# A bidirectional Mamba written as four fixed lists of stages, one per engine

## The chip, the cores and the metric

One core of one Trainium2 chip runs the whole kernel in one launch. The metric is the device time of that core in microseconds (us), less is better. In the profile PE is TensorE (PEld its weight loads), DVE is VectorE, ACT is ScalarE, POOL is GpSimd, SP is SyncE with the DMA queues.

## The reference, cut to what matters

The input x has 4 sequences of 1024 tokens with 128 channels. It goes through a layer norm, a Mamba in both directions (forward on the tokens, backward on the reversed tokens, each with its own weights, the two outputs averaged and added to the residual), and then six layers of a local-attention transformer. One Mamba direction, with 256 inner channels and 16 states:

```python
def _mamba(x, W_in, W_conv, b_conv, W_x, W_dt, b_dt, A_log, Dp, W_out):
    xp, z = jnp.split(x @ W_in.T, 2, axis=-1)
    xc = silu(causal_depthwise_conv4(xp, W_conv) + b_conv)
    dt, Bm, Cm = jnp.split(xc @ W_x.T, [DT_RANK, DT_RANK + D_STATE], axis=-1)
    dt = jax.nn.softplus(dt @ W_dt.T + b_dt)
    A = -jnp.exp(A_log)
    # for every token t, with h of shape (256, 16):
    #   h = h * exp(dt_t * A) + (dt_t * xc_t) * B_t ;  y_t = sum over states of h * C_t
    y = ys + xc * Dp
    y = y * jax.nn.silu(z)
    return y @ W_out.T
```

The transformer is not shown; the change doesn't alter what it issues.

## The kernel before

Channels lie on the 128 partitions and tokens along the free dimension, so the 256 inner channels are two halves h = 0, 1. One pass s is one direction of one sequence (8 passes, even ones forward, odd ones backward). A pass has 16 steps n, one for each state; g = 16 s + n counts steps over the whole block, 128 of them. A step works on all 1024 tokens at once:

- TensorE spreads row n of B over all partitions with a matmul against a picked column (`b_rows`, through `rows`, L209) into a pair of PSUM banks, and row n of C (`c_rows`) into the other pair. ScalarE copies C to SBUF (`copy_c`, L316).
- ScalarE makes the decays exp(dt A_n) of both halves (`decays`, L309), up to four steps ahead.
- VectorE multiplies dt*xc by B for half 0 into the tile drive (L393) and for half 1 in place in PSUM (L395), and then runs one scan over the tokens for each half (L411), into one of four buffers of state.
- GpSimd multiplies each scanned state by C into read (L425).
- TensorE adds each read to y of its half with the identity as weights, in PSUM, over the 16 states (`add_read`, L229). y takes four of the eight banks for the whole block.

Once a pass come the projections of the next pass (`project` on TensorE, `take_projection` on ScalarE): x with the four taps of the convolution folded into the weights (L182), z (L188), x_dbl, which holds B, C and the low-rank dt (L196), and dt (L203), then softplus as Abs, Relu, Exp and Ln on ScalarE and a sum and a product on VectorE (L353, L360). B is split into a rounded and a low part (L346). At the end of a pass VectorE adds the skip term (L366, the old y in PSUM plus D times xc), multiplies by silu(z) (`gate`, L372), TensorE multiplies by W_out (L238), and VectorE adds half of the result to the residual (`add_output`, L380).

The order is written out in the loops: the tables say in which step each projection stands, in most cases for the whole 1024 tokens at once.

```python
PROJECT_AT = {1: ("x", 0, BOTH), 4: ("x", 1, [0]), 6: ("x", 1, [1]), 8: ("bc", 0, BOTH), 9: ("dt", 0, BOTH),
              10: ("dt", 1, BOTH), 12: ("z", 0, BOTH), 13: ("z", 1, BOTH)}
GATE_AT, OUTPUT_AT, SOFTPLUS_AT, SPLIT_AT, DT_AT, DTX_AT = 1, 2, 11, 10, 12, 14
LEAD_DECAYS = 3
```

The other four banks are two pairs, `slot[0]` and `slot[1]`. B of step g goes to `slot[g % 2]`; C of step g and the projection of step g go to `slot[(g + 1) % 2]`, one after the other, and B of step g+1 to the same one behind them. `take(q, now)` makes TensorE wait for the last reader of the pair. Each engine runs its instructions strictly in the order written.

## Time and profile before

| | before |
|---|---|
| median of 3 runs | 4172.57 us (4169.62 to 4175.07) |
| profiled execution: its time, its span | 4178.99 us, 4176.9 us |
| busy over the span: PE, DVE, ACT, POOL | 3828.7 (92%), 3409.8 (82%), 3048.1 (73%), 3035.9 (73%) us |
| granted TensorE clock, mean | 0.952 of full speed |
| Mamba block: TensorE's first matmul to the last output sum | 71.45 to 1232.35 us |

Busy is the time in which an engine has an instruction in work; the records of matmuls overlap a little at their ends. The granted clock is a mean over a stretch of two levels, 1.0 (2.4 GHz) and 0.5 (1.2 GHz). In lists of groups a row ends with the idle time of the engine just before those instructions and with what released them.

### The profile page before, as it was taken

Reading aid. Unit: us, or ns where it says so; the run is one execution under the profiler, and the core shown is the slowest. Engines: PE = TensorE matmul, PEld = TensorE weight load, DVE = VectorE, ACT = ScalarE, POOL = GpSimd, SP = SyncE. Lnnn points to the kernel's source line nnn. Section 1 sums busy time; section 2 is a strip of 40 time slices with the busy share of each in tenths; the row PEclk is TensorE's granted clock in tenths of the full one; section 3 lists DMA queues with packets and bytes.
Section 4 is the critical chain, followed back from the end, with each engine's and each line's share of the span. In section 5 each row is a group of like instructions: output and inputs, shape, how many; then the busy total and the mean of one; then the engine's idle time right before and its main releaser. Section 6 shows DMA issues by size and latency. Waiting matters only on the chain.

```text
span 4176.9 us, 110200 instructions
## 1 busy us (share of the span) xinstructions
PE 3828.7 (92%) x43616; PEld 2570.0 (62%) x43616; DVE 3409.8 (82%) x3480; ACT 3048.1 (73%) x6956; POOL 3035.9 (73%) x2330
## 2 busy tenths in 40 slices
PE   6788888888875999999999999999999999999998
PEld 2333333333333777777777777777777777777775
DVE  3788888888975888788887888788887888788885
ACT  4655645564534888788887888788887888788885
POOL 0455555554546888888888888888888888888883
PEclk8888898898887999999999999999999999999999
DMA  1000000000000000000000000000000000000001
GB/s 41 0 1 0 0 0 0 0 0 0 0 20 32 13 2 15 2 6 13 15 3 2 16 2 15 2 6 12 2 15 2 16 2 15 2 6 2 3 2 42
DMA packets 12012, 34.46 MB, mean 8 GB/s; under 512 B 2405, under 2 KB 4329, under 8 KB 10609
## 3 DMA queue, kind: packets, MB, share of 16 engines
q1 hardware_dynamic: 11504, 27.41, 1.9%
q8 instruction: 353, 5.78, 0.6%
q14 instruction: 155, 1.26, 0.1%
HBM read 23.21 MB, written 4.19 MB: 7 GB/s over the span
## 4 chain that ended last, share of the span: by engine, by line
PE 64%; issue 2%; ACT 1%; POOL 1%; DVE 0%; POOLq 0%; ACTq 0%; DVEq 0%
PE ps L849 16%; PE ps L779 12%; PE ps L838 9%; PE ps L790 8%; PE ps L826 6%; PE ps L874 5%; PE ps L887 3%; PE ps L811 1%; PE ps L801 1%; PE ps L856 1%; PE ps L862 1%; ACT prob L980 0%; PE ps L761 0%; ACT mixed L989 0%; POOL resid L1257 0%
## 5 line engine op out<-in xcount | busy, mean ns | idle before, releaser
L425 POOL TENSOR_TENSOR read<-state,c_row 128x1024 f32<-128x1024 f32 x256 | 598.9, 2359 | 620.7 <-DVE state L411 501.0
L1235 POOL TENSOR_TENSOR resid<-resid,sq 128x1024 f32<-128x1024 f32 x384 | 909.8, 2375 | 4.0 <-DVE sq L1089 3.7
L1257 POOL TENSOR_TENSOR resid<-resid,rnorm 128x1024 f32<-128x1024 f32 x384 | 725.5, 1905 | 17.8
L849 PE MATMUL ps<-mixed,w_vo 128*128 128x128 f32 x6144 | 718.6, 275 | 3.0 <-ACT mixed L989 2.3
L849 PEld LDWEIGHTS ps<-mixed,w_vo 128*128 128x128 f32 x6144 | 709.6, 192 | 12.9 <-issue 4.6
L779 PE MATMUL ps<-w_qk,xs_parts 128*128 128x512 f32 x2304 | 641.3, 414 | 47.3 <-issue 18.2
L980 ACT ACTIVATE prob<-ps,stat 128x64 f32<-128x64 f32 x3072 | 653.3, 384 | 1.1 <-DVE stat L1109 1.1
L229 PE MATMUL mamba_ps<-read,ident 128*128 128x512 f32 x1024 | 572.0, 697 | 22.4 <-DVE xc L366 19.8
L1089 DVE TENSOR_TENSOR sq<-ps,rope_l 128x1024 f32<-128x1024 f32 x384 | 462.7, 1205 | 119.1 <-ACT sq L942 118.8
L1102 DVE TENSOR_TENSOR resid<-ps,rope_l 128x1024 f32<-128x1024 f32 x384 | 464.5, 1210 | 74.6 <-ACT sq L942 67.5
L779 PEld LDWEIGHTS ps<-w_qk,xs_parts 128*128 128x128 f32 x2304 | 414.8, 192 | 164.0 <-issue 81.1
L942 ACT ACTIVATE sq<-ps 128x1024 f32<-128x1024 f32 x384 | 395.7, 1030 | 162.3 <-PE ps L779 127.0
L1264 POOL TENSOR_TENSOR prob<-prob,stat 128x1024 f32<-128x1024 f32 x192 | 366.2, 1907 | 174.9 <-DVE stat L1120 174.8
L989 ACT COPY mixed<-ps 128x512 f32<-128x512 f32 x768 | 399.5, 601 | 110.5 <-PE ps L838 110.5
L1066 DVE TENSOR_REDUCE ssq<-sq 128x16 f32<-128x1024 f32 x384 | 465.7, 1213 | 8.1 <-ACT sq L942 3.7
L790 PE MATMUL ps<-ident,resid 128*128 128x128 f32 x3072 | 413.9, 274 | 14.3 <-ACT w_vo L924 13.1
L229 PEld LDWEIGHTS mamba_ps<-read,ident 128*128 128x128 f32 x1024 | 209.1, 217 | 311.6 <-issue 262.1
L790 PEld LDWEIGHTS ps<-ident,resid 128*128 128x128 f32 x3072 | 350.9, 141 | 75.8 <-issue 61.1
L838 PE MATMUL ps<-prob_t,rows 32*128 32x512 f32 x3072 | 383.8, 613 | 4.2 <-DVE xb L1137 1.6
L316 ACT COPY c_row<-mamba_ps 128x1024 f32<-128x1024 f32 x128 | 128.4, 1003 | 270.9 <-PE mamba_ps L209 270.9
L964 ACT COPY q_t<-ps 128x512 f32<-128x512 f32 x384 | 230.4, 600 | 124.0 <-PE ps L790 121.7
L826 PE MATMUL ps<-k_t,q_t 64*32 64x64 f32 (+1 forms) x24576 | 291.6, 225 | 9.8 <-issue 9.3
(139 smaller groups left out, 6158.5 us busy)
## 6 DMA issues: line engine op xcount, KB each, us to landing
w_stage<-w_qk_hbm SPq DMA_DIRECT2D x6, 1024.0 KB, 4.9
vo_stage<-w_v_hbm SPq DMA_DIRECT2D x6, 512.0 KB, 3.8
vo_stage<-w_o_hbm SPq DMA_DIRECT2D x6, 512.0 KB, 4.6
xn<-x_hbm SPq DMA_DIRECT2D x4, 512.0 KB, 5.3
kept<-resid SPq DMA_DIRECT2D x8, 256.0 KB, 3.1
resid<-kept SPq DMA_DIRECT2D x8, 256.0 KB, 4.5
out_hbm<-resid SPq DMA_DIRECT2D x8, 256.0 KB, 2.0
w_stage<-w_hbm SPq DMA_DIRECT2D x6, 341.0 KB, 2.9
```

What stands on the lines that cost most here:

```text
L229: last = pe.matmul(y_ps[h][:, c, :], ident[:, :], read[:, (2 * g + h) % 4, c * BANK:(c + 1) * BANK], start=n == 0, stop=n == D_STATE - 1)
L425: pool.tensor_tensor(read[:, u % 4, :], state[:, u % 4, :], c_row[:, (u // 2) % 2, :], ALU.mult).then_inc(read_ready, 1)
L779: last = pe.matmul(ps[:, A + c, :], xs_parts[:, odd, xpart, :], w_qk[:, wpart, cols], start=k == 0, stop=k == 2)
L790: last = pe.transpose(bank[:, j * P:(j + 1) * P], qk[:, tile % 2, col:col + P], ident[:, :])
L826: last = pe.matmul(ps[w * WINDOW:(w + 1) * WINDOW, S + h, first:(a + 1) * 2 * WINDOW], q_t[rows_h, odd, a, w * WINDOW:(w + 1) * WINDOW], k ...
L838: last = pe.matmul(banks[w], rows[rows_w, tile % 2, own, :], prob_t[rows_w, tile % 2, :, own, :], start=own == 0, stop=own == 1)
L849: last = pe.matmul(bank[:, 0:P], w_vo[:, l % 2, head_at(place_h), :], mixed[:, odd, place_h, :], start=place_h == 0, stop=place_h == HEADS ...
L980: last = act.activation(prob[:, tile % 2, place_h, :], score_ps[:, place_h, :], ACT.Exp, bias=stat[:, tile % 2, 0, place_h:place_h + 1])
L1066: dve.tensor_reduce(ssq[:, tile % 2, part * HEADS:(part + 1) * HEADS, 0], sq[:, 0, :].rearrange("p (h d) -> p h d", d=HEAD_DIM), AX_X, ALU ...
L1102: dve.tensor_tensor(qk[:, tile % 2, part * INNER:(part + 1) * INNER].rearrange("p (h d) -> p h d", d=HEAD_DIM), heads_ps.rearrange("p (h d ...
L1235: pool.tensor_tensor(qk[:, tile % 2, cols], qk[:, tile % 2, cols], sq[:, 1 + part, :], ALU.add).then_inc(done[f"rotated{part}"], 1)
L1257: pool.tensor_tensor(heads, heads, norms, ALU.mult).then_inc(done[f"normed{part}"], 1)
```

## The change

The loops of the Mamba block are replaced by four lists, MAMBA_PE, MAMBA_ACT, MAMBA_DVE and MAMBA_POOL. An entry is (lag, step, stage): in round i the stage is issued for pass i - lag, so that work of up to three passes stands between one another in a list (`mamba_sequence`). Every stage waits for what it reads and for the last reader of what it overwrites (`after`, by counts taken from the lists).

- The four banks of the two pairs are given by `mamba_slots`: B still takes a whole pair, alternately; every other result (half of C, of x, z, x_dbl, dt or the output) takes one bank of the pair that B does not hold, the two in turn.
- C is spread and copied in two halves of 512 tokens (c0, c1; cc0, cc1), so are all projections and their reads, and the output with its sum (o0, o1; ao0, ao1).
- ScalarE reads x with Identity (bias added) and z with Copy, in halves, and then puts the whole of each channel half through Silu in SBUF (sx0, sx1, sz0, sz1). After a group of Silus it preloads the table set with Exp and Ln; one such preload stands at the start.
- Skip (gs0, gs1) and gate (gm0, gm1) stay on VectorE, as separate stages per half, and the identity sums (y0, y1) lag behind the scans by up to three steps.
- state and read have two buffers per half where they had four in turn. The semaphore `stored` of the transformer is allocated in `program` instead.

```diff
+MAMBA_PE = [
+    (2, 13, "c0"), (2, 13, "c1"), (2, 11, "y0"), (2, 14, "c0"), (2, 14, "b"), (2, 14, "c1"), (2, 12, "y0"), (2, 15, "b"),
+    (2, 11, "y1"), (2, 12, "y1"), (2, 15, "c1"), (2, 13, "y0"), (2, 15, "c0"), (2, 14, "y0"), (2, 13, "y1"), (1, 0, "b"),
+    (1, 0, "c1"), (2, 14, "y1"), (1, 0, "c0"), (2, 15, "y0"), (1, 1, "b"), (0, None, "x01"), (2, 15, "y1"),
+    (0, None, "x00"), (1, 1, "c1"), (1, 1, "c0"), (1, 2, "c1"), (1, 0, "y0"), (1, 2, "b"), (1, 2, "c0"), (2, None, "o0"),
+    (2, None, "o1"), (0, None, "z10"), (1, 0, "y1"), (1, 3, "b"), (1, 1, "y0"), (1, 3, "c0"), (1, 3, "c1"), (1, 2, "y0"),
+    (1, 4, "c1"), (1, 1, "y1"), (1, 4, "b"), (0, None, "x10"), (1, 4, "c0"), (1, 2, "y1"), (1, 5, "b"), (1, 3, "y0"),
+    (1, 5, "c1"), (0, None, "x11"), (1, 5, "c0"), (1, 4, "y0"), (1, 6, "b"), (1, 6, "c0"), (1, 3, "y1"), (1, 6, "c1"),
+    (1, 4, "y1"), (0, None, "z00"), (1, 7, "b"), (1, 7, "c0"), (0, None, "z01"), (1, 5, "y0"), (0, None, "z11"),
+    (1, 7, "c1"), (1, 5, "y1"), (1, 8, "b"), (1, 8, "c1"), (0, None, "bc1"), (1, 8, "c0"), (1, 6, "y1"), (1, 9, "b"),
+    (1, 6, "y0"), (1, 9, "c0"), (0, None, "bc0"), (0, None, "dt01"), (0, None, "dt00"), (1, 7, "y1"), (1, 10, "b"),
+    (1, 9, "c1"), (1, 8, "y1"), (1, 10, "c0"), (0, None, "dt11"), (1, 10, "c1"), (1, 7, "y0"), (1, 8, "y0"),
+    (1, 11, "b"), (1, 9, "y1"), (1, 11, "c1"), (1, 11, "c0"), (1, 9, "y0"), (1, 12, "b"), (1, 12, "c0"),
+    (0, None, "dt10"), (1, 12, "c1"), (1, 10, "y0"), (1, 10, "y1"), (1, 13, "b")]
+MAMBA_ACT = [
...
+    (2, 4, "cc1"), (1, None, "sx0"), (2, 6, "dec1"), (1, None, "ax10"), (2, 4, "cc0"),
...
+    (2, 6, "cc0"), (2, 6, "cc1"), (1, None, "sx1"), (1, None, "az00"), (2, 7, "cc0"), (1, None, "az01"),
+    (1, None, "sz0"), (2, None, "sz1"), (2, 7, "cc1"), (1, None, "az11"), (2, 9, "dec0"), (2, 8, "cc1"), (2, 8, "dec1"),
...
+MAMBA_DVE = [
+    (2, 14, "sc0"), (2, 14, "sc1"), (2, 15, "dr0"), (2, 15, "dr1"), (2, 15, "sc0"), (2, 15, "sc1"), (1, None, "tx1"),
+    (1, 0, "dr0"), (1, 0, "dr1"), (1, 0, "sc1"), (1, 0, "sc0"), (2, None, "gs0"), (1, 1, "dr0"), (2, None, "gm0"),
+    (1, 1, "dr1"), (2, None, "gs1"), (1, 1, "sc1"), (1, 1, "sc0"), (2, None, "gm1"), (1, 2, "dr0"), (1, 2, "dr1"),
+    (2, None, "ao0"), (1, 2, "sc0"), (2, None, "ao1"), (1, 2, "sc1"), (1, 3, "dr0"), (1, 3, "dr1"), (1, 3, "sc1"),
...
+    (1, 9, "dr0"), (1, 9, "dr1"), (1, 9, "sc1"), (1, 9, "sc0"), (0, None, "split"), (1, 10, "dr0"), (1, 10, "dr1"),
+    (1, 10, "sc0"), (1, 10, "sc1"), (1, 11, "dr0"), (1, 11, "dr1"), (1, 11, "sc0"), (1, 11, "sc1"), (0, None, "ar0"),
+    (1, 12, "dr0"), (1, 12, "dr1"), (1, 12, "sc0"), (1, 12, "sc1"), (0, None, "tx0"), (1, 13, "dr0"), (1, 13, "dr1"),
+    (1, 13, "sc1"), (1, 13, "sc0"), (0, None, "ar1"), (1, 14, "dr0"), (1, 14, "dr1")]
...
+def mamba_sequence(order):
+
+    out = []
+    for i in range(2 * BATCH + max(lag for lag, _, _ in order)):
+        for lag, n, name in order:
+            if 0 <= i - lag < 2 * BATCH:
+                out.append((name, i - lag if n is None else D_STATE * (i - lag) + n))
+    return out
...
+    slots, last, turn, pair = {}, [None] * 4, [0, 0], 1
+    for name, k in pe:
+        if name == "b":
+            pair = k % 2
+            banks, reader = [2 * pair, 2 * pair + 1], ("sc1", k)
+        elif name in single:
+            other = 1 - pair
+            banks, reader = [2 * other + turn[other]], (single[name], k)
+            turn[other] ^= 1
+        else:
+            continue
+        slots[name, k] = banks[0], sorted({last[q] for q in banks if last[q]})
+        for q in banks:
+            last[q] = reader
...
+        def after(eng, *producers):
+
+            for name, k in producers:
+                if k >= 0:
+                    eng.wait_ge(done[name], COUNT[name, k])
...
+                act.preload_act_table_set("natural_log_exp_and_others")
...
+                def copy_c(c):
+                    def stage(g):
+                        after(act, (f"c{c}", g), ("rd0", g - 2), ("rd1", g - 2))
+                        act.copy(c_row[:, g % 2, cols(c)], bank(f"c{c}", g)).then_inc(done[f"cc{c}"], 1)
+                    return stage
...
+                for i, (name, k) in enumerate(ACT_SEQ):
+                    stages[name](k)
+                    tables = [x[0] for x in ACT_SEQ[i + 1:] if x[0] in MAMBA_EXPS + MAMBA_SILUS]
+                    if name in MAMBA_SILUS and tables and tables[0] in MAMBA_EXPS:
+                        act.preload_act_table_set("natural_log_exp_and_others")
...
+                def scan(h):
+                    def stage(g):
+                        after(dve, (f"dec{h}", g), (f"dr{h}", g), (f"rd{h}", g - 2))
+                        force = pair(g).rearrange("p c n -> p (c n)") if h else drive[:, :]
+                        dve.tensor_tensor_scan(state[:, h, g % 2, :], decay[:, h, g % AHEAD, :], force,
+                                               0.0, ALU.mult, ALU.add).then_inc(done[f"sc{h}"], 1)
+                    return stage
```

## Rows read from the trace of the kernel before

**Rows 1.** Windows of the whole span by stage: busy time and instructions per engine, granted clock.
```profile
661.00:798.00 137.00, 118.49 (x243) 47.60 (x243) 114.08 (x70) 73.65 (x70) 72.13 (x31) 0.86 0.00 0
...
1400.00:4177.00 2777.00, 2709.32 (x40072) 2086.17 (x40072) 2302.21 (x2705) 2293.90 (x6077) 2334.21 (x1978) 0.99 0.03 9
```

**Rows 2.** Timeline of two steps without a projection, last pass: start, length, engine, operation.
```profile
1196.65 1.20 DVE L393 TENSOR_TENSOR drive<-dtx,mamba_ps 128x1024 f32<-128x1024 f32 x1
...
1197.45 3.90 PE L229 MATMUL mamba_ps<-read,ident 128*128 128x512 f32 x8
...
1203.56 1.19 DVE L393 TENSOR_TENSOR drive<-dtx,mamba_ps 128x1024 f32<-128x1024 f32 x1
```

**Rows 3.** Groups by line and shape, from 0 to 1500 us.
```profile
L229 PE MATMUL mamba_ps<-read,ident 128*128 128x512 f32 x1024 | 572.0, 697 | 22.4 <-DVE xc L366 19.8 <-POOL read L425 2.6
...
L209 PE MATMUL mamba_ps<-bc,pick_r 64*128 64x512 f32 x512 | 179.2, 447 | 131.2 <-DVE state L411 112.8 <-ACT c_row L316 14.5 <-ACT dtx L291 3.0
...
L309 ACT ACT_TABLE_LOAD x43 | 55.2, 1283 | 0.8
...
L277 ACT ACT_TABLE_LOAD x22 | 28.2, 1283 | 42.7 <-DVE zs L372 31.6 <-PE mamba_ps L182 10.8
...
L353 DVE TENSOR_TENSOR dt<-dt,dtx 128x1024 f32<-128x1024 f32 x16 | 20.1, 1295 | 15.2 <-ACT dt L300 15.2
L366 DVE SCALAR_TENSOR_TENSOR xc<-xc,packed,mamba_ps 128x1024 f32<-128x1024 f32 x16 | 19.8, 1275 | 4.5 <-PE mamba_ps L229 4.5
...
L360 DVE TENSOR_TENSOR dtx<-dt,xc 128x1024 f32<-128x1024 f32 x16 | 19.0, 1228 | 0.0
L372 DVE TENSOR_TENSOR zs<-xc,zs 128x1024 f32<-128x1024 f32 x16 | 18.8, 1218 | 0.0
...
L277 ACT ACTIVATE xc<-mamba_ps,packed 128x512 f32<-128x512 f32 x16 | 11.0, 687 | 53.8 <-PE mamba_ps L182 53.8
...
L380 DVE SCALAR_TENSOR_TENSOR resid<-mamba_ps,resid 128x1024 f32<-128x1024 f32 x8 | 9.8, 1225 | 19.4 <-PE mamba_ps L238 19.4
L346 DVE TENSOR_TENSOR bc<-x_dbl,bc 32x1024 fp32r<-32x1024 f32 x8 | 9.7, 1215 | 22.7 <-ACT bc L286 22.5
```

**Rows 4.** Waits from 100 to 1400 us: who waited for whom, us, times, longest.
```profile
DVE drive L393 <- PE mamba_ps L209: 125.3, 54, 7.0
...
DVE resid L380 <- PE mamba_ps L238: 19.4, 8, 4.4
```

**Rows 5.** Timeline of a step with a projection, pass 5.
```profile
714.94 3.59 PE L182 MATMUL mamba_ps<-xn,wtap 128*128 128x512 f32 x8
...
720.18 1.20 PE L209 MATMUL mamba_ps<-bc,pick_r 64*128 64x512 f32 x4
...
720.94 1.22 DVE L393 TENSOR_TENSOR drive<-dtx,mamba_ps 128x1024 f32<-128x1024 f32 x1 [1.62 <-PE mamba_ps L209]
```

**Rows 6.** Windows of 4 us, columns as in group 1.
```profile
677.00:681.00 4.00, 0.73 (x2) 0.29 (x2) 3.97 (x4) 1.01 (x1) 3.70 (x2) 0.82 0.00 0
681.00:685.00 4.00, 3.24 (x4) 1.51 (x5) 4.00 (x4) 0.00 (x0) 0.00 (x0) 0.50 0.00 0
...
689.00:693.00 4.00, 4.00 (x11) 1.75 (x10) 0.54 (x1) 0.08 (x1) 3.11 (x2) 1.00 0.00 0
```

**Rows 7.** Timeline of the preamble of the Mamba block.
```profile
71.45 15.93 PE L182 MATMUL mamba_ps<-xn,wtap 128*128 128x512 f32 x32 [15.37 <-DVE wtap L336]
...
104.79 1.28 ACT L297 ACT_TABLE_LOAD   x1
...
106.08 2.00 ACT L297 ACTIVATE dt<-dt 128x1024 f32<-128x1024 f32 x2
...
115.22 1.22 DVE L393 TENSOR_TENSOR drive<-dtx,mamba_ps 128x1024 f32<-128x1024 f32 x1
```

**Rows 8.** Timeline of the end of the Mamba block.
```profile
1215.20 2.25 DVE L411 TENSOR_TENSOR_SCAN state<-decay,mamba_ps 128x1024 f32<-128x1024 f32 x1
...
1231.12 1.23 DVE L380 SCALAR_TENSOR_TENSOR resid<-mamba_ps,resid 128x1024 f32<-128x1024 f32 x1 [4.39 <-PE mamba_ps L238]
```

More of the change, by code:

```diff
@@ L258, in _, with free, project_x, stage @@
-                for h in range(HALVES):
-                    add_read(STEPS - 1, h)
-                output(PASSES - 1, other_slot(STEPS - 1))
+                def free(name, k):
+                    after(pe, *SLOTS[name, k][1])
+                    return bank(name, k)
+                def project_x(h, c):
+                    def stage(s):
+                        to, d = free(f"x{h}{c}", s), s % 2
+                        for tap in reversed(range(D_CONV)):
+                            skip = max(0, D_CONV - 1 - tap - c * BANK)
+                            seen = tokens(s, c * BANK + skip - (D_CONV - 1 - tap), BANK - skip)
+                            last = pe.matmul(to[:, skip:], wtap[:, d, tap, h * P:(h + 1) * P], seen,
+                                             start=tap == D_CONV - 1, stop=tap == 0)
+                        last.then_inc(done[f"x{h}{c}"], 1)
+                    return stage
@@ new lines, in project_z, with stage, project_bc @@
+                def project_z(h, c):
+                    def stage(s):
+                        to = free(f"z{h}{c}", s)
+                        pe.matmul(to, win[:, s % 2, D_INNER + h * P:D_INNER + (h + 1) * P], tokens(s, c * BANK, BANK),
+                                  start=True, stop=True).then_inc(done[f"z{h}{c}"], 1)
+                    return stage
+                def project_bc(c):
+                    def stage(s):
+                        after(pe, ("sx0", s), ("sx1", s))
+                        to = free(f"bc{c}", s)
+                        for h in range(HALVES):
+                            last = pe.matmul(to[0:BC_ROWS + DT_RANK], wx[:, s % 2, h, :], xc[:, s % 2, h, cols(c)],
+                                             start=h == 0, stop=h == HALVES - 1)
+                        last.then_inc(done[f"bc{c}"], 1)
+                    return stage
@@ new lines, in b_rows, with c_rows @@
+                def b_rows(g):
+                    after(pe, ("split", g // D_STATE))
+                    free("b", g)
+                    for c in range(HALF_BANKS):
+                        last = rows(pair(g)[:, c, :], g, g % D_STATE, c)
+                    last.then_inc(done["b"], 1)
+                def c_rows(c):
+                    def stage(g):
+                        after(pe, ("split", g // D_STATE))
+                        rows(free(f"c{c}", g), g, D_STATE + g % D_STATE, c).then_inc(done[f"c{c}"], 1)
+                    return stage
@@ new lines, in output, with stage @@
+                def output(c):
+                    def stage(s):
+                        after(pe, ("gm0", s), ("gm1", s))
+                        to = free(f"o{c}", s)
+                        for h in range(HALVES):
+                            last = pe.matmul(to, wout[:, s % 2, h, :], zs[:, s % 2, h, cols(c)], start=h == 0, stop=h == HALVES - 1)
+                        last.then_inc(done[f"o{c}"], 1)
+                    return stage
+                stages = {**parts("x", project_x), **parts("z", project_z), **parts("dt", project_dt), **banked("bc", project_bc),
+                          "b": b_rows, **banked("c", c_rows), **halved("y", add_read), **banked("o", output)}
@@ L429 @@
+                stages = halved("rd", read_out)
+                for name, k in POOL_SEQ:
+                    stages[name](k)
 DEPTH, HEADS, HEAD_DIM, WINDOW = 6, 16, 64, 32
```

418 lines of the change are left out of this document (178 added, 240 removed), and 20 rows, old and new, of tables (MAMBA_ACT, MAMBA_DVE, MAMBA_POOL).

## The prediction

> **What bounds the kernel now.** I read the windows by stage first. The Mamba block is the part before 1232 us; from 1400 us on, the transformer keeps TensorE at 2709 of 2777 us at a granted clock of 0.99 [rows 1], and the diff touches nothing there that takes time (the semaphore `stored` is only allocated earlier). So 2,945 us of the 4,177 are the same in both kernels, and I ask only about Mamba. A typical window there has 137 us, of which VectorE is busy 114, TensorE 118 (at clock 0.86), ScalarE 74 and GpSimd 72 [rows 1]. Two engines are near full and neither is full: that is a pair of engines waiting for each other in turn.
>
> The timeline says which is the floor. In a step without a projection, the drive of half 0 comes back after 1203.56 - 1196.65 = 6.91 us, with nothing idle on VectorE (two drives and two scans), and TensorE has time left [rows 2]. At that pace 128 steps take 884.5 us. To them come the operations that occur once a pass: relu sum, product with xc, skip, gate, output sum and split, together 20.1 + 19.0 + 19.8 + 18.8 + 9.8 + 9.7 = 97.2 us, 12.15 a pass [rows 3]. Seven passes of these lie between the first drive at 115.22 [rows 7] and the end of the last scan at 1215.20 + 2.25 = 1217.45 [rows 8]: 85.1 us. VectorE alone would need 884.5 + 85.1 = 969.6 us; the stretch takes 1102.2. **132.6 us are stalls**, 137.8 us a pass where 122.7 would do at full packing. The view of waits names them: the drive waits 125.3 us for the B rows of L209, and the output sum 19.4 us for L238, 4.4 of it at the very end [rows 4, 8].
>
> Why are the B rows late? A pair of banks holds B(g-1) until its second scan ends. Then C(g), a whole projection and B(g+1) go through this same pair one behind the other, each after the ScalarE read of the one before. With a projection, eight matmul records take 3.59 us, and the next B comes 1.62 us late [rows 5]. I take 0.44 us for a record of 512 columns at full clock (3.59/8, a little off for the last one's drain), and 0.30 for a record of the row matmuls (1.20/4). The clock adds to it: TensorE is busy 0.73 of 4 us, the clock falls to 0.50 while VectorE is still fully busy, and two windows on VectorE is busy 0.54 of 4 us, waiting [rows 6]. Half speed is not paid in the light step where it arises, but in the heavy one that follows.
>
> **The change part by part.** *TensorE.* The same matmuls: 192 records a pass of 512 columns (128 of the identity sum, 1024 in all [rows 3], 32 of x, 8 each of z, bc, dt and output), and 64 row records [rows 3]. That is 192 x 0.44 + 64 x 0.30 = 103.7 us at full clock, against VectorE's 122.7. What moves is where they stand. A projection is now one bank (x 3.5 us, output and bc 1.8, z and dt 0.9), C is split in two single banks, and a turn within the pair lets one be computed while ScalarE reads the other. The identity sums lag up to three steps, so TensorE has work where it used to wait. I walked the steps of MAMBA_PE with these durations, t = 0 where the other pair comes free. B is ready at 4 to 5 us in steps 3, 4, 8 and 11, of the 6.9 that VectorE gives; at 6.2 to 6.6 in steps 5, 6 and 10; near 7.1 in step 7 (z01, z11 and sz0, sz1 of ScalarE). Steps 1, 2, 9 and 12 hold the most, and there VectorE has its extra 1.2 to 5 us (gs0, gm0, gs1, gm1; two ao; split; ar0 and tx0), so B is in time by 1 to 2 us. That leaves under 1 us of stall a pass at full clock. One record at half clock costs 0.44 more, and steps 5, 6, 7 and 10 have no more than 0.7 to spare; one such stretch a pass costs some 2 us. I take **3 us a pass, 22 in all**, between 0 and half of the present stalls, 66.
>
> *VectorE.* Same operations in the same number, except that the output sum is cut in two. No row shows a 512-wide output sum; ScalarE's reads cost 0.69 for 512 columns, so two are 1.38 where VectorE's whole one is 1.23 [rows 3]. That is 0.15 more a pass, 1 us. Drives now name their operands as two banks of 512; the same 1024 elements lie in the same order, so I put 0, and if it did cost, the difference of the two kinds of drive-like operation here (1.23 against 1.30 [rows 3]) times 256 bounds it at 18 us. The scan's order (half 1 first in some steps) costs nothing of itself; GpSimd follows in the same order.
>
> *ScalarE.* More reads, in halves: C twice 0.6 to 0.69 for 1.0, x and z read first by Identity or Copy and then put through Silu in SBUF. That adds some 5 us of C, 2.5 of x, 2.5 of z and 1 of dt, say 11 a pass. Fewer table loads: sx0 stands alone, sx1, sz0 and sz1 share one, and a preload of the set with Exp and Ln follows each group, so four a pass where 88 stand now (43 and 22 of them in two rows [rows 3]): 11 a pass, so minus 7 x 1.28 = 9 us. ScalarE goes from about 75 to under 80 of 122.7 us: not a bound, hidden behind VectorE, as GpSimd's 72 is [rows 1]. But it is a strict list, and its waits (dec for the scan four back, cc for rd two back, abc for the previous dt) now hold what stands behind them: the worst place is sx1, load and Silu 2.3 us before az00, for which B of step 7 waits.
>
> On the price of a load the trace and the Trainium skill differ. In the preamble the load takes 1.28 us, and the activation starts at 106.08, right behind it [rows 7]. ScalarE: Activation LUTs, section "What ACT_TABLE_LOAD costs", has the same load and a drain of 1.38 us besides. By the page seven loads fewer would be 19 us of ScalarE a pass and not 9; the measurement decides, and since ScalarE is covered either way the sum is the same.
>
> *The preamble.* TensorE starts at 71.45 and the first drive at 115.22 [rows 7]. In the new list ScalarE's items of pass 0 up to the first decays are 16 halves of 0.69, 9 whole ones of about 1.1 and two loads of 1.28: 23.5 us. The first x bank before them, the waits of bc and dt on each other, and add, product and drive behind them add some 8. That gives 103 to 105 if no turn is missed. The gain lies between 2.6 (two loads) and 13; I take **10**, since nothing covers a new wait here.
>
> *The end.* From the last scan to the last output sum it is now 1232.35 - 1217.45 = 14.9 us [rows 8]. The gate of half 0 moves ahead of the skip of half 1, and the first bank of the output is added while the second is computed: **2** less, between 0 and 4.
>
> Sum: 132.6 - 22 - 1 + 10 + 2 = 121.6, rounded to 122. The profiled execution took 4178.99 us with its span of 4176.9, so 2.1 lie around it, and it is 6.4 over the median of 4172.57; the gain is 2.9% either way. 4172.6 - 122 = **4050 us**.
>
> **The rivals.** *(A) Only half the stalls go (0.15).* If the lists, whose slack is 0.3 to 0.7 us in four steps, meet the clock's falls, each pass keeps 8 of its 16 us of waits. For it: those falls are in the present rows [rows 6]. Against it: TensorE's work is spread. 66 + 10 = 76: 4097 us.
>
> *(B) The bound moves and nothing is gained (0.03).* B would have to be late by 16 us a pass, 1 us in every step, with ScalarE's added reads as the cause. It would need ScalarE near full, and it has over 40 us a pass free. 4173 us.
>
> *(C) TensorE becomes the bound and the kernel gets slower (0.05).* One mechanism: pieces of one bank, each behind a wait for its reader, leave TensorE so many short gaps that the clock stays low. TensorE needs 103.7 us over the clock; it equals today's 137.8 at a clock of 0.75, and above that point it does not decide. At 0.70 it takes 148 a pass, plus 10 x 8: 4255 us. The rows give 0.86 with gaps of 3 us and more [rows 1, 6], and the new list has less idle time to share out, so a small chance. The Trainium skill has this as a rule: TensorE: Matmul & The Clock Gate, "A second HAM failure mode: psum-queue depth-cycling", tells of a kernel that went through its banks in turn and whose clock swung because of short idle times between groups. By that rule (C) would happen; the trace agrees that the clock swings, but shows it after gaps of several us.
>
> *(D) No stall remains (0.07).* 132.6 - 1 + 13 + 4 = 149: 4024 us, the least that VectorE's floor allows.
>
> **How the numbers follow.** The forecast has 0.70: 4050, by itself 4030 to 4073 (1 to 6 us of stall a pass). The range takes in (D) and (A): 4023 to 4098. What a measurement of this kernel can tell from no change is about 0.2%, 8 us. Forecast, (A) and (D) are faster: 0.92. (B) is the same: 0.03. (C) is slower, 0.05.
>
> **What would show it.** After: a pass of 123 to 127 us between like scans; VectorE busy 96% of a window in the passes; its wait for the B rows 125.3 -> about 20; the clock in a pass at 0.93 or more; some 33 table loads in Mamba; first drive at about 105; the transformer from its start to its end as long as before. It would be wrong if waits of VectorE appear elsewhere (for `dec`, `rd` or `y`), if ScalarE is over 95 us a pass, or if the clock in the passes is under 0.8.

## The result, and the profile after

The changed kernel takes 4157.19 us (median of 7 runs, 4147.51 to 4162.93) against 4174.53 of the kernel before on the same chips: a ratio of 0.9959, 95% interval 0.9945 to 0.9972. It is faster by 0.4%, where 2.9% was forecast, and lies far above the range. The profiled execution has a span of 4161.1 us, 15.8 less than before.

Cut at the same four places in both traces (first drive of half 0, end of the last scan, end of the last output sum, end), the spans stand like this; the last column is the sum of the prediction:

```
                                   before     after    change   forecast
start to first drive               115.22    111.30      -3.9      -10
first drive to last scan          1102.23   1052.35     -49.9     -109.6
last scan to last output sum        14.90     16.24      +1.3       -2
last output sum to the end        2944.51   2981.16     +36.7        0
span                              4176.9    4161.1      -15.8     -121.6
```

Mamba's steps gave less than half of what was expected, and the transformer, in which no arithmetic is changed, became 37 us longer.

**The windows by stage**, to be read beside [rows 1] (columns as there):

```profile
661.00:798.00 137.00, 122.84 (x264) 47.60 (x265) 129.30 (x79) 76.52 (x96) 93.50 (x33) 0.94 0.00 0
...
1400.00:4161.00 2761.00, 2666.97 (x39391) 2048.89 (x39389) 2265.40 (x2660) 2245.70 (x5956) 2285.91 (x1942) 0.99 0.03 8
```

In the pass VectorE is now busy 129 us of 137 (94%, where 96% was forecast), and TensorE has a granted clock of 0.94, as forecast. But GpSimd is busy 94 us, where it was 72, for about as many reads (33 and 31 instructions in the windows).

**VectorE's waits**, to be read beside [rows 4]:

```profile
DVE drive L471 <- PE mamba_ps L307: 51.4, 43, 4.7
DVE state L479 <- ACT decay L417: 8.2, 7, 1.6
```

The wait for the B rows fell from 125.3 to 51.4 us, and 8.2 for the decays came up; 22 had been allowed.

**The groups by line and shape**, with the instruction's mean in ns after the busy time:

```profile
L521 POOL TENSOR_TENSOR read<-state,c_row 128x1024 f32<-128x1024 f32 x256 | 725.8, 2856 | 442.0 <-DVE state L479 246.4 <-PE mamba_ps L330 104.3 <-ACT c_row L424 90.8
...
L479 DVE TENSOR_TENSOR_SCAN state<-decay,drive 128x1024 f32<-128x1024 f32 x128 | 322.8, 2522 | 0.0
L479 DVE TENSOR_TENSOR_SCAN state<-decay,mamba_ps 128x1024 f32<-128x1024 f32 x128 | 290.1, 2267 | 11.0 <-ACT decay L417 8.2 <-POOL read L521 0.4
...
L495 DVE TENSOR_TENSOR zs<-xc,zs 128x1024 f32<-128x1024 f32 x16 | 34.1, 2134 | 0.1
```

The same groups in the kernel before:

```profile
L425 POOL TENSOR_TENSOR read<-state,c_row 128x1024 f32<-128x1024 f32 x256 | 598.9, 2359 | 620.7 <-DVE state L411 501.0 <-ACT c_row L316 119.7
...
L411 DVE TENSOR_TENSOR_SCAN state<-decay,drive 128x1024 f32<-128x1024 f32 x128 | 299.5, 2340 | 0.2
L411 DVE TENSOR_TENSOR_SCAN state<-decay,mamba_ps 128x1024 f32<-128x1024 f32 x128 | 289.1, 2259 | 0.0
```

GpSimd's read took 2359 ns before, now 2856. The scan of half 0, all of whose operands are in SBUF, took 2340, now 2522. The scan of half 1, whose force is in PSUM, is where it was (2259, now 2267). And the gate, two SBUF operands as well, went from 1218 [rows 3] to 2134. Nothing in the diff changes what these instructions do.

**The timeline at step 3 and step 4 of one pass** shows what an instruction is waiting for when it is long:

```profile
670.94 2.29 DVE L479 TENSOR_TENSOR_SCAN state<-decay,mamba_ps 128x1024 f32<-128x1024 f32 x1
...
675.49 4.68 POOL L521 TENSOR_TENSOR read<-state,c_row 128x1024 f32<-128x1024 f32 x2 [2.59 <-DVE state L479]
...
677.81 4.51 DVE L479 TENSOR_TENSOR_SCAN state<-decay,drive 128x1024 f32<-128x1024 f32 x1
...
682.25 2.25 DVE L479 TENSOR_TENSOR_SCAN state<-decay,mamba_ps 128x1024 f32<-128x1024 f32 x1
```

The scan of half 1 comes first in step 3 on VectorE, but GpSimd's list has the read of half 0 first there. So GpSimd starts its two reads at 675.49, once both scans are over, and they last until 680.17. VectorE's next scan of half 0 begins at 677.81 and takes 4.51 us: 2.28 and the 2.2 until GpSimd is done. An engine that waits for a semaphore shows idle time; this one shows a longer instruction.

Which engine pays is not fixed here. In step 4 this scan and GpSimd's second read start within 0.02 us of each other in all eight passes. In five of them the scan took 4.5 us and the read 2.35; in the other three the scan took 2.28 and the read 4.43.

**The timeline of one step in which no VectorE instruction is lengthened**, between two drives of half 0 (the scans take 2.28 and 2.26 us; it is GpSimd's read beside them that takes 4.41):

```profile
755.41 1.21 DVE L471 TENSOR_TENSOR drive<-dtx,mamba_ps 128x1024 f32<-128x1024 f32 x1
...
762.05 1.20 DVE L471 TENSOR_TENSOR drive<-dtx,mamba_ps 128x1024 f32<-128x1024 f32 x1
```

6.64 us, where [rows 2] had 6.91. Part of that 6.91 had been waits too. In the kernel before each half-1 drive waited for the half-0 drive before it to be finished (a start-to-start of 1.24 us, now 1.13). And the half-0 scan of that one step was 0.15 us longer than 2.28, beside a read that lasted until 1199.31:

```profile
1199.03 2.43 DVE L411 TENSOR_TENSOR_SCAN state<-decay,drive 128x1024 f32<-128x1024 f32 x1
```

The commonest step of the kernel before took 6.77 us.

**The preamble and the end:**

```profile
71.84 9.20 PE L276 MATMUL mamba_ps<-xn,wtap 128*128 128x512 f32 x16 [15.36 <-DVE wtap L440]
...
77.72 0.69 ACT L360 ACTIVATE xc<-mamba_ps,packed 128x512 f32<-128x512 f32 x1 [6.29 <-PE mamba_ps L276]
...
111.30 1.22 DVE L471 TENSOR_TENSOR drive<-dtx,mamba_ps 128x1024 f32<-128x1024 f32 x1
```

The first bank of x is in ScalarE's hands 5.9 us after TensorE's start, and ScalarE then waits for TensorE before each of the other three x banks too (2.67, 0.66 and 2.75 us); the prediction had some 8 us for the first bank and all waits up to the first drive. The end:

```profile
1161.39 2.26 DVE L479 TENSOR_TENSOR_SCAN state<-decay,mamba_ps 128x1024 f32<-128x1024 f32 x1
...
1161.54 8.85 PE L330 MATMUL mamba_ps<-read,ident 128*128 128x512 f32 x20
...
1168.71 1.28 DVE L487 SCALAR_TENSOR_TENSOR xc<-xc,packed,mamba_ps 128x1024 f32<-128x1024 f32 x1 [5.05 <-PE mamba_ps L330]
...
1179.20 0.69 DVE L508 SCALAR_TENSOR_TENSOR resid<-mamba_ps,resid 128x512 f32<-128x512 f32 x1 [2.25 <-PE mamba_ps L340]
```

Five groups of lagging sums (20 records) stand in front of the skip, which begins 5.1 us after the last scan.

**The transformer.** A run of 128 matmuls of 64 columns (L826 before, L927 after) in the changed kernel:

```profile
1290.79 1.12 PE L927 MATMUL ps<-k_t,q_t 64*32 64x64 f32 x91
1293.14 0.63 PE L927 MATMUL ps<-k_t,q_t 64*32 64x64 f32 x37 [1.23 <-issue]
```

Nothing is being waited for (issue), yet TensorE stands still for 1.23 us between two equal instructions. TensorE's waits that end in "issue" on this line, over the whole transformer, after and before (us in total, times, longest):

```profile
PE ps L927 <- issue: 37.5, 39, 1.9
```

```profile
PE ps L826 <- issue: 9.3, 22, 1.8
```

Counted in all of TensorE's records (weight loads, matmuls and the waits between them), these pauses stand at one place in every 256: within the runs of 64-column matmuls no other instruction starts more than 0.4 us behind the one before it. I summed the start-to-start times in front of the instructions of one residue modulo 256, over the transformer: the median over all residues is 11.0 to 11.3 us in these traces; at the residue with the pauses it is 28.9 us before and 64.2 after. The difference, 35.3, is nearly all of the transformer's 36.7. Most boundaries cost nothing: of the 192 that fall into such runs 40 cost more than 0.3 us (26 before), and none of these lies in the first two thirds of a run. In the last fifth they cost 1.0 us on average, 0.3 before; some stand just behind a run, in front of L939 (up to 1.4 us).

### The profile page after: what moved, and what is told of

It reads as the page before. It is cut to its first block, busy times and chain, and to the rows that moved or that the text cites. A ratio compares the mean times of both kernels' runs of the same rounds, so it can differ in the third digit from the quotient of the medians.

```text
span 4161.1 us, 111723 instructions
## 1 busy us (share of the span) xinstructions
PE 3836.6 (92%) x43616; PEld 2552.7 (61%) x43616; DVE 3442.0 (83%) x3488; ACT 3023.3 (73%) x7123; POOL 3160.4 (76%) x2330
## 4 chain that ended last, share of the span: by engine, by line
PE 65%; issue 2%; ACT 1%; POOL 1%; DVE 0%; POOLq 0%; ACTq 0%; DVEq 0%
PE ps L950 16%; PE ps L880 13%; PE ps L939 9%; PE ps L891 8%; PE ps L927 6%; PE ps L975 5%; PE ps L988 3%; PE ps L912 1%; PE ps L902 1%; PE ps L957 1%; PE ps L963 1%; ACT prob L1081 0%; PE ps L862 0%; ACT mixed L1090 0%; POOL resid L1358 0%
## 5 line engine op out<-in xcount | busy, mean ns | idle before, releaser
L521 POOL TENSOR_TENSOR read<-state,c_row 128x1024 f32<-128x1024 f32 x256 | 725.8, 2856 | 442.0 <-DVE state L479 246.4
L950 PEld LDWEIGHTS ps<-mixed,w_vo 128*128 128x128 f32 x6144 | 708.2, 192 | 12.7 <-issue 4.6
L330 PE MATMUL mamba_ps<-read,ident 128*128 128x512 f32 x1024 | 546.0, 665 | 2.7 <-POOL read L521 2.7
L1043 ACT ACTIVATE sq<-ps 128x1024 f32<-128x1024 f32 x384 | 395.2, 1029 | 168.4 <-PE ps L880 136.5
L424 ACT COPY c_row<-mamba_ps 128x512 f32<-128x512 f32 x256 | 145.8, 583 | 362.7 <-PE mamba_ps L307 312.4
L939 PE MATMUL ps<-prob_t,rows 32*128 32x512 f32 x3072 | 389.1, 615 | 7.2 <-issue 3.2
L330 PEld LDWEIGHTS mamba_ps<-read,ident 128*128 128x128 f32 x1024 | 192.9, 204 | 240.1 <-issue 232.3
L927 PE MATMUL ps<-k_t,q_t 64*32 64x64 f32 (+1 forms) x24576 | 294.3, 225 | 37.6 <-issue 37.5
L479 DVE TENSOR_TENSOR_SCAN state<-decay,drive 128x1024 f32<-128x1024 f32 x128 | 322.8, 2522 | 0.0
```

Source lines behind the costliest of these rows:

```text
L330: last = pe.matmul(y_ps[h][:, c, :], ident[:, :], read[:, h, g % 2, cols(c)], start=n == 0, stop=n == LAST)
L521: pool.tensor_tensor(read[:, h, g % 2, :], state[:, h, g % 2, :], c_row[:, g % 2, :], ALU.mult).then_inc(done[f"rd{h}"], 1)
L927: last = pe.matmul(ps[w * WINDOW:(w + 1) * WINDOW, S + h, first:(a + 1) * 2 * WINDOW], q_t[rows_h, odd, a, w * WINDOW:(w + 1) * WINDOW], k ...
L939: last = pe.matmul(banks[w], rows[rows_w, tile % 2, own, :], prob_t[rows_w, tile % 2, :, own, :], start=own == 0, stop=own == 1)
L950: last = pe.matmul(bank[:, 0:P], w_vo[:, l % 2, head_at(place_h), :], mixed[:, odd, place_h, :], start=place_h == 0, stop=place_h == HEADS ...
```

## The experiments

Segments of all runs, cut as above. "Pauses" is the sum at every 256th instruction, "shift" how many instructions stand in front of the transformer more than in the kernel before, modulo 256.

```
                      first    to last   to output   to the   pauses  shift
                      drive     scan       sum         end            mod 256
before               115.22   1102.23     14.90     2944.51    28.9      0
after                111.30   1052.35     16.24     2981.16    64.2    150
e1 short reads       110.47   1007.83     16.25     2977.40    57.2    150
e2 straight order    111.88   1100.21     20.07     2977.09    55.5    150
e3 clear of reads    112.16   1096.99     20.35     2977.16    60.1    150
e4 after, +106       119.91   1045.71     16.25     2936.12    20.2      0
e5 before, +150      116.10   1102.36     14.91     2985.85    59.6    150
e6 after, +106       110.75   1039.37     15.53     2939.84    23.0      0
e7 gate moved, +106  111.07   1018.84     16.39     2938.95    22.4      0
e8 short sums        109.30   1024.87     10.86     2983.39    63.3    150
e9 B first, +106     109.97   1033.96     17.55     2943.20    23.5      0
e10 after, +256      109.55   1048.77     16.26     2997.76    60.1    150
e11 after, +234      109.27   1041.65     13.83     2990.37    59.9    128
e12 B13 first, +106  109.50   1010.30     17.40     2942.07    24.6      0
```

Each line is one trace. In five of them Mamba's instructions are the same (after, e4, e6, e10, e11), and its stretch from the first drive to the last scan lies between 1039.4 and 1052.4 us. A part of that spread is step 4 above: the scan is the one that waits in 5, 1, 1, 4 and 4 of the 8 passes. So a difference of less than 13 us between two such stretches doesn't show an effect.

### The transformer: e4, e5, e6, e10, e11

The instructions put in are waits on a semaphore that has long been raised; two of them make one instruction.

```diff
 # e5: in the kernel before; e6, e10, e11: in the changed kernel, with 212, 512, 468
         @block.tensor
         def _(pe):
+            for _ in range(300):
+                pe.wait_ge(GATE[0], 2)
```

**e4**: the same in front of Mamba's first matmul, 212 waits.

> The changed kernel with 106 instructions more on TensorE's queue (waits on a semaphore long satisfied) before its first matmul of Mamba, where it waits 15 us for the taps. With the 406 that the change adds, the transformer's instructions are then shifted by 512, a multiple of 256, against the kernel before. In both traces the transformer's extra idle time stands at every 256th instruction of TensorE (28.9 us before, 64.2 after, against 11.0 at any other residue). Theory F1 (where the transformer's instructions lie against these blocks of 256 decides): the time from the last output sum of Mamba to the end goes from 2981 back to about 2945 us, total about 4121. Theory F2 (the length of these pauses hangs on something else, such as where the program lies in memory or the single execution): it stays within 10 us of 2981, or moves without regard to the shift.

4120.40 us, ratio to before 0.9870 (0.9856 to 0.9885). The rest fell by 45 us to 2936.12, and the pauses by 44.0; 8.6 us went to the instructions themselves, which outlasted the idle time before the first drive.

> The kernel before with 150 instructions more on TensorE's queue, at the very start of the transformer, where it waits over 25 us for weights (so they lie in idle time): waits on a semaphore long satisfied. 150 is what the change's 406 leave modulo 256. Theory F1 (the position against the blocks of 256 decides): the time from the last output sum of Mamba to the end goes from 2945 to about 2980 us, and the kernel is 30 to 40 us slower, about 4208, with Mamba as before. Theory F2 (a property of the changed program or of its place in memory): no change, 4173.

4218.11 us, ratio 1.0104 (1.0088 to 1.0119). The kernel before, with nothing but 150 more instructions in idle time (the first projection starts 0.3 us later than without them), loses 41 us in the transformer, and Mamba stays at 1102.4. 30.7 of the 41 stand at the boundaries; the other 10 are spread over the transformer and not explained. Its pauses on this line (L831 there):

```profile
PE ps L831 <- issue: 34.1, 34, 1.8
```

> The changed kernel with the 106 instructions at the start of the transformer, in idle time, and not before Mamba's first matmul, where they put the first drive off by 8 us. Theory F1: rest 2936 to 2945 us as in the run with the shift before Mamba, first drive back at 111, total 4112 to 4116. F2: about 4157.

4108.02 us, ratio 0.9843 (0.9825 to 0.9862), 49 us below the changed kernel's median. In the traces the rest is 41.3 us shorter and the pauses 41.2; another 13 stand in Mamba, where nothing is changed. The pauses on the same line (L932 there):

```profile
PE ps L932 <- issue: 4.8, 10, 1.8
```

> The changed kernel with 256 instructions at the start of the transformer on TensorE's queue. Theory F1 (position modulo 256): nothing changes against the changed kernel, rest 2977 to 2986 us and the idle time at each 256th instruction 55 to 65 us. Theory F3 (position modulo more than 256, or simply any shift from the present place): the rest falls to about 2940.

> The changed kernel with 234 instructions there, half a block (128) beyond e6. Theory F1 says only that 64 and 60 us stood at a shift of 150 modulo 256 and 20 to 29 at a shift of 0, so a shift of 128 should give a value near that of 150: 45 to 65 us at each 256th instruction and a rest of 2965 to 2985.

e10: 4174.11 us in one run, pauses 60.1. A whole block of 256 leaves them as they were, so the residue counts. Its rest, expected as before, is 16.6 us over that of the changed kernel. 11.8 of them are there because the first projection of the transformer starts 61.6 us after the last output sum and not 49.8: the 256 instructions, one every 0.107 us, last longer than the idle time. e11: 4156.91 us in one run, pauses 59.9, first projection at 59.2, so its rest is 5 us over the expected 2985 as well. A shift of half a block is as bad as one of 150; only the position of the kernel before was good, of the three that were tried.

Theory F1 holds in both directions and F2 and F3 fall: two programs with the same arithmetic differ by some 40 us in the transformer by where its TensorE instructions lie against blocks of 256. Why boundaries in the last fifth of a run cost 0.3 us at one position and 1.0 at the other, though about as many of them fall there (35 and 38), no run shows.

### GpSimd and VectorE: e1

```diff
-                        pool.tensor_tensor(read[:, h, g % 2, :], state[:, h, g % 2, :], c_row[:, g % 2, :],
+                        pool.tensor_tensor(read[:, h, g % 2, 0:64], state[:, h, g % 2, 0:64], c_row[:, g % 2, 0:64],
                                            ALU.mult).then_inc(done[f"rd{h}"], 1)
```

The one memset of read that the run also has is not shown.

> The changed kernel, but GpSimd's 256 reads multiply 64 of the 1024 columns (the other columns of the read tile stay at 0 from one memset before), so y is not computed in full; all else, the waits too, is the same. Theory P (a VectorE instruction with two SBUF inputs and a GpSimd multiplication of two SBUF operands exclude each other, and each waits for the other in turn; the late reads then make the identity sums and B late): the half-0 scan goes from 2.52 us back to 2.28 and the gate from 2.13 to 1.2, VectorE's wait for the B rows falls from 51 us to under 20, and the stretch from first drive to last scan falls from 1052 us to about 985. Theory Q (B is late because of TensorE's own list and its clock, and the long VectorE instructions only fill time that would be waited out): the durations fall as well, but the waits for B grow by as much, and the stretch stays above 1035.

4111.87 us, ratio 0.9851 (0.9832 to 0.9871). The half-0 scan by form, and VectorE's wait for B:

```profile
L479 DVE TENSOR_TENSOR_SCAN state<-decay,drive 128x1024 f32<-128x1024 f32 x128 | 291.7, 2279 | 0.0
```

```profile
DVE drive L471 <- PE mamba_ps L307: 61.5, 51, 4.6
```

The scan is back at 2279 ns, the gate at 1211, and the stretch is 44.5 us shorter. That is theory P's first half. Its second half is wrong: the wait for B did not fall to under 20 us but rose to 61.5, and the stretch is 1008, not 985. Theory Q foresaw the waits and put the stretch too high. So the long instructions cost about 45 us and were not hidden: VectorE's instructions in the stretch add up to 44.6 us less, while its waits of over 0.15 us stay at 63 in total (10 more for B, 10 less for decays and outputs).

And B is late by itself as well. For step 6, with 12.7 of the 61.5 us, this trace shows why. A window from the drive of step 5 to that of step 6 (columns as in [rows 1]):

```profile
405.46:414.09 8.63, 8.63 (x21) 3.33 (x19) 6.70 (x6) 3.16 (x5) 0.64 (x2) 1.00 0.00 0
```

TensorE is busy in all of the 8.63 us, at a granted clock of 1.00, while VectorE needs 6.70 of them. It is the same in three other passes. The list gives TensorE more to do before this B than the step lasts.

### The order of the scans and the gate: e2, e3, e7

```diff
 # e2: steps 0, 1, 3, 9 and 13 of MAMBA_DVE, MAMBA_POOL to match
-    (1, 0, "sc1"), (1, 0, "sc0")
+    (1, 0, "sc0"), (1, 0, "sc1")
 # e3: besides e2; the first three lines are also e7, there with (1, 1, "sc1"), (1, 1, "sc0") kept
-    (2, None, "gs0"), (1, 1, "dr0"), (2, None, "gm0"), (1, 1, "dr1"), (2, None, "gs1"), ... (2, None, "gm1"),
+    (1, 1, "dr0"), (2, None, "gs0"), (1, 1, "dr1"), (2, None, "gs1"), (2, None, "gm0"), (2, None, "gm1"), ...
+    MAMBA_PE: (1, 1, "b"), (2, 15, "y1"), (0, None, "x01")
+    MAMBA_PE: (1, 4, "b"), (1, 2, "y1"), (0, None, "x10"); (1, 9, "c0"), (1, 9, "c1"), (0, None, "bc0")
+    MAMBA_ACT: (2, 9, "cc0"), (2, 9, "cc1"), (2, 9, "dec1")
```

> The changed kernel with the scans of half 0 before those of half 1 in all steps (five steps a pass had them the other way), and GpSimd's reads in the same order. Theory P: in a step with half 1 first, the read of half 1 can't start while the scan of half 0 runs, both reads stand behind it and meet the next half-0 scan; in order, the reads fall under the half-1 scan and the drives, which have a PSUM operand. The half-0 scan falls to under 2.4 us and the stretch by 20 to 35 us, total about 4130. Theory Q: half 1 first frees the PSUM pair 2.2 us earlier for the x banks of steps 1 and 4 and for step 10, so B comes later in these steps: waits for B grow by up to 2.2 us in three steps a pass, and the total is 4150 to 4180.

> As the straight order, and besides: skips and gates stand after the drives of step 1 (dr0, gs0, dr1, gs1, gm0, gm1), where both reads are over; y1 of the last step goes ahead of x01, y1 of step 2 ahead of x10; both halves of C of step 9 are made before B of step 10. Theory P: the gate is back at 1.2 to 1.3 us, VectorE's total excess is under 10 us, waits for B under 20: stretch 990 to 1010, total 4105 to 4125. Theory Q: total as with the straight order alone, within 8 us.

e2: 4208.06 us, ratio 1.0083 (1.0068 to 1.0098). e3: 4207.18, ratio 1.0082 (1.0065 to 1.0099). Both are slower than the kernel before, and my theory about the order falls. The half-0 scan and the gate in e3:

```profile
L479 DVE TENSOR_TENSOR_SCAN state<-decay,drive 128x1024 f32<-128x1024 f32 x128 | 355.8, 2780 | 0.0
...
L495 DVE TENSOR_TENSOR zs<-xc,zs 128x1024 f32<-128x1024 f32 x16 | 18.8, 1219 | 0.0
```

The gate is at 1219 ns, because it stands where no read runs; but the half-0 scans became longer, 2780 ns, not shorter. Summed over the passes, their excess over 2280 ns is 31 us in the changed kernel, 52 in e2 and 64 in e3. The straight order doesn't take GpSimd's reads from under the half-0 scans, because they are late for another reason too: GpSimd waits for the identity sums that free its buffers, 104.3 us in the changed kernel, 168.4 in e2 and 200.6 in e3. These sums stand in TensorE's list behind the x banks, which in e2 get their PSUM pair one scan later; that this is the link is argued from the lists and not shown by a run. The five swapped steps are not the fault of the change; taken back without the rest of the plan, they cost 48 us of the stretch.

> As e6, and in step 1 skips and gates stand after the drives (dr0, gs0, dr1, gs1, gm0, gm1), y1 of the last step goes ahead of x01; the scans keep the change's order, half 1 first in five steps. Theory P with its first part alone (what the gate waits for GpSimd is lost on VectorE's path): gate from 2.13 to 1.2 us, 15 us less than e6. Theory Q' (VectorE's time saved there comes back as a wait for B, since TensorE and ScalarE have little to spare in the steps behind): gate 1.2 us, total within 5 us of e6.

4090.09 us, ratio 0.9799 (0.9785 to 0.9814), against e6's 4108.02 on the same chip. The gate is at 1217 ns and the stretch 20.5 us shorter than e6's. Theory P holds here, Q' falls: the 18 us between the medians are at least the 14.6 that the 16 gates had lost. The sum y1 that e7 also moves ahead of x01 was not tested by itself.

### TensorE's work: e8

```diff
 # e8: besides e1
-                            last = pe.matmul(y_ps[h][:, c, :], ident[:, :], read[:, h, g % 2, cols(c)],
+                            w = BANK if n == 0 else 64
+                            last = pe.matmul(y_ps[h][:, c, 0:w], ident[:, :], read[:, h, g % 2, c * BANK:c * BANK + w],
```

> As e1 (GpSimd multiplies 64 columns), and TensorE's identity sums take 64 of 512 columns except in the first state of a pass, so both y and the output are not computed; TensorE then has some 45 us less work a pass. In e1 VectorE still waited 61 us for the B rows. If these waits are TensorE's work (theory T), they fall under 15 us and the stretch from first drive to last scan from 1008 to 950 to 965. If they are ScalarE's list and its waits (theory A), they stay above 40 and the stretch above 990.

4130.19 us in one run, 18 more than e1 with less work. A window of one pass (columns as in [rows 1]) and the wait for B:

```profile
250.00:387.00 137.00, 110.76 (x276) 56.32 (x274) 125.97 (x81) 79.31 (x101) 16.62 (x33) 0.68 0.00 0
```

```profile
DVE drive L472 <- PE mamba_ps L307: 71.6, 51, 4.6
```

The wait rose from 61.5 to 71.6 us, and the stretch to 1024.9. The granted clock fell to 0.68 from e1's 0.94: TensorE, with less to do, was at 1.2 GHz for most of the window. Neither T nor A can be read from that; the run doesn't separate TensorE's work from ScalarE's list, because it changed the clock.

### B behind the sums: e9, e12

The wait for B by step in e7, summed over the passes (all idle time of VectorE before the half-0 drive, gaps under 0.15 us too, which the view of waits leaves out): step 13 has 19.3 of 53.9 us, step 6 has 11.5. The timeline of e7 at step 13:

```profile
715.35 16.74 POOL L524 TENSOR_TENSOR read<-state,c_row 128x1024 f32<-128x1024 f32 x5 [2.68 <-PE mamba_ps L333]
...
729.31 6.28 PE L333 MATMUL mamba_ps<-read,ident 128*128 128x512 f32 x8
...
733.26 2.35 POOL L524 TENSOR_TENSOR read<-state,c_row 128x1024 f32<-128x1024 f32 x1 [1.17 <-PE mamba_ps L333]
...
735.51 1.19 PE L310 MATMUL mamba_ps<-bc,pick_r 64*128 64x512 f32 x4
...
736.28 1.22 DVE L474 TENSOR_TENSOR drive<-dtx,mamba_ps 128x1024 f32<-128x1024 f32 x1 [3.04 <-PE mamba_ps L310]
```

GpSimd ends the fifth of its reads at 732.09 and needs 3.35 us for each, where a free one takes 2.36. TensorE's sums from 729.31 on contain y1 of step 10, which waits for it, and B of step 13 (735.51) stands behind. VectorE drives at 736.28, 3.04 us late.

```diff
 # e9 and e12: MAMBA_PE
-    (1, 10, "y0"), (1, 10, "y1"), (1, 13, "b")]
+    (1, 10, "y0"), (1, 13, "b")]       and (2, 10, "y1") at the head of the list
 # e9 alone
-    (1, 5, "c0"), (1, 4, "y0"), (1, 6, "b"),
+    (1, 5, "c0"), (1, 6, "b"), (1, 4, "y0"),
```

> As e7, and on TensorE's list B of step 13 stands ahead of y1 of step 10, and B of step 6 ahead of y0 of step 4. In the trace of e7 these two steps hold 19.3 + 11.5 of VectorE's 54 us of waits for B, and in step 13 TensorE stands at y1 of step 10, whose read GpSimd delivers late (five reads in 16.7 us for 11.8), with B ready to be made behind it. Theory P (late reads hold up B through TensorE's order): the waits in steps 6 and 13 fall from 31 to under 10 us and the total from 4090 by 12 to 22, to 4068 to 4078. Theory A (the reader of B's bank on ScalarE, relu10 or ax11, comes as late anyway): the waits stay above 20 and the total within 5 us of e7.

4106.51 us, ratio 0.9818 (0.9797 to 0.9839). Step 13 is down to 1.0 us and step 6 to 5.7, but step 7 rose from 4.7 to 18.6, and the excess of the half-0 scans from 16.3 to 32.5. The expected 12 to 22 us did not come; what two waits gave stands in other places. One of its five runs took 4083.96 us, the others 4104 to 4107.

> As e7, with only B of step 13 ahead of y1 of step 10 (the other exchange of e9, in step 6, is taken back). In e9 the wait in step 13 fell from 19.3 to 1.0 us, that in step 7 rose from 4.7 to 18.6, and the excess of the half-0 scans rose from 16 to 33 us. If the exchange in step 6 was to blame for both (its y0 came later, and GpSimd's reads with it), this kernel keeps 15 us of e7's waits and comes to 4072 to 4080. If VectorE, going on earlier in step 13, only meets GpSimd's late reads in its next scans (theory P: the two engines hand the delay to one another), the excess in steps 13 and 14 rises by some 14 us as in e9 and the total stays within 5 us of 4090.

4081.05 us (4071.34 to 4096.35), ratio 0.9776 (0.9756 to 0.9796), the lowest median of all, but its interval overlaps that of e7. VectorE's wait for B in e7 and in e12:

```profile
DVE drive L474 <- PE mamba_ps L310: 50.3, 41, 4.7
```

```profile
DVE drive L474 <- PE mamba_ps L310: 27.3, 29, 4.6
```

23.0 us less are waited for B, the excess of the half-0 scans is 9.7 us more (26.0), and the stretch is 8.5 us shorter. Step 13's wait is gone, and step 7's is at 4.6 us, as in e7: the exchange in step 6 was to blame for e9's step 7. A part of what step 13 gave went to longer scans, as theory P has it. Whether the kernel gained anything over e7 is not shown: 8.5 us is less than the 13 by which equal stretches differ.

## Why the prediction was wrong

**The step that failed most is the first one**, "the diff touches nothing there that takes time", so that "2,945 us of the 4,177 are the same in both kernels". The rest is 36.7 us longer. The 406 instructions (waits) that Mamba's lists add on TensorE's queue shift all that follows, and e4, e5, e6 and e10 show that the shift alone does it. That is shown, and it took 36.7 of the 52.5 us that the change gained up to the last output sum. No rival had it.

The Trainium skill has the blocks: Runtime: NRT & Kernel Launch, section "Instruction fetch mechanics", says that instructions are fetched in blocks of 256 and that crossing a boundary is mostly hidden. The period of 256 agrees with these traces, and so does the word mostly, since 152 of the 192 boundaries inside the runs cost less than 0.3 us. The others do not agree with hiding: 1.23 us of standstill in the rows above, and at this residue 53 us more than at the median one. That the fetch is what TensorE stands still for is the page's account; no run shows it.

**The second is the cover of GpSimd**: "not a bound, hidden behind VectorE, as GpSimd's 72 is". GpSimd is no bound, but it was not free either. With the reads where the new lists put them, VectorE's half-0 scans and gates were 46 us longer in all (128 scans by 0.24 us over 2.28, 16 gates by 0.92), and e1 got 44.5 us of stretch back by making the reads short. The kernel before had hidden this by its fixed order, in which a read fell under the half-1 scan and the drives; 0.06 us a scan was all that showed, as 2340 ns on a scan whose undisturbed time is 2280, and I had taken it as the scan's own length.

A premise of the prediction was wrong here too: "GpSimd follows in the same order". In steps 1, 3 and 13 VectorE's list has half 1 first and GpSimd's has half 0 first, so that both reads stand behind both scans, as in the timeline of step 3. No run swaps GpSimd's order alone; in e2, which straightens all orders, the scans of step 4 lose their excess (11.1 to 2.2 us), but they do so in e4 and e6 as well, with nothing changed.

The Trainium skill states this: SBUF — State Buffer, section "Who interferes with whom": a VectorE instruction with two SBUF inputs contends with a GpSimd instruction that reads SBUF, and one waits for the whole of the other. The trace agrees: 4.51 us for a 2.28 us scan beside 4.68 us of reads, and 2.27 for the scan with a PSUM operand. The prediction should have weighed it; by it the reads' positions against the two-input operations belonged into the walk.

**The third is the size of "3 us a pass, 22 in all"**: the waits for B came to 51.4 and for decays to 8.2. The clock was as forecast (0.94), but the walk was wrong in single steps. It has B of step 6 ready at 6.2 to 6.6 us; in e1 TensorE is busy 8.63 us up to it at full clock, 1.9 over what VectorE gives. And it names no late read: in step 13, with 19.1 us of the 51, the sum of a late read stood in front of B on TensorE's list, and with short reads (e1) 11.7 of them remain. What the other waits of e1's 61.5 us hang on is open, since e8 moved the clock.

**What went the other way**: VectorE's floor was not 6.91 us a step but 6.64. The step in [rows 2] had a lengthened scan and a drive that waited. Over 128 steps the difference is 35 us, and it hid a part of the other two errors, by luck: 128 x 6.64 + 7 x 12.15 (the operations once a pass, as in the prediction) = 935 us, plus 46 of long instructions, plus 59.6 of waits, is 1041 of the 1052 measured; 11 us are in small gaps that I didn't assign.

**Preamble and end** were mis-sized: 3.9 us for 10, and a loss of 1.3 for a gain of 2. The first 16 matmuls of the x banks took 575 ns each (9.20 us in all), where the prediction has 0.44 us, and the lagged sums stand in front of the last skip.

Of the rivals, (A) came nearest in Mamba (half of the stalls gone) but for another reason and without the transformer's loss. (C), the clock, didn't happen, and neither did the transfer of the bound to ScalarE (76 us in a window of 137). The 33 table loads are there (1 + 16 + 16), and they changed nothing that can be seen.

## What to carry to other kernels

A change in one part moves the instructions of all later parts; when a later part that was not touched has another length, look for pauses at a fixed period in TensorE's stream, and shift it by some instructions placed in idle time before judging the change. Ask of every pair of VectorE and GpSimd instructions that may overlap whether both read two SBUF operands, and take an instruction's median and maximum, not its mean, for its price: the spread of 2.28 to 4.5 us in equal scans was a wait in disguise. In a strict list each exchange that ends a wait lets other engines run into each other elsewhere, so sum the whole stretch, not the step, and know first by how much equal stretches differ (13 us here).

## What was not expected of the hardware

- TensorE stands still for up to 2.15 us at boundaries of 256 instructions, in the last third of a run of 64-column matmuls or just behind it, and in the last fifth for 0.3 or 1.0 us on average depending on the program's position.
- A scan and a GpSimd read that start within 0.02 us of each other exclude one another, and in the same kernel now the one waits (scan 4.5 us), now the other (read 4.43 us).
- With work taken from TensorE the kernel was 18 us slower (e8, one run, against e1): the granted clock in a pass went from 0.94 to 0.68.
- VectorE's two drives of a step, without a wait between them, start 1.13 us apart where each reports 1.21 to 1.22 us.
